# First stage of a two-layer cross-attention and mixture-of-experts kernel, rewritten without engine loops

## What is computed

```
x = x + L0_xattn(layernorm(x), ctx)          # A: cosine of every pair of tokens
    v = xn @ Wv.T + bv                       # 128 -> 64
    t = ctx @ Wt.T + bt                      # 96 -> 64, "the text side"
    out[i, j] = (v_i . t_j) / max(|v_i| |t_j|, 1e-8)
x = x + L0_ffn(layernorm(x))                 # B: routed experts
    logits = xn @ gate_w ; 8 experts in 4 groups, 2 groups, then 2 experts kept
    y = sum of the chosen experts' silu(xn @ w_gate) * (xn @ w_up) @ w_down, and a shared one
```

## Time and profile before

| what | value |
|---|---|
| median of 3 runs | 867.25 us (865.78 to 868.15) |
| profiled execution | span 862.7 us, 26300 instructions; its own time is not listed apart from the span |
| busy in the span | PE 727.4, PEld 545.5, DVE 639.6, ACT 408.4, POOL 198.2 us |
| mean granted TensorE clock | 0.931 of 2.4 GHz |
| first stage | 0 to 255.0 us of the span |

### The profile page before, as it was taken

How to read it: one execution, slowest core, us unless ns; L and a number is a source line. 1 busy time by engine, 2 the same in 40 slices (tenths; PEclk the granted TensorE clock), 3 DMA queues, 4 the chain that set the end, 5 groups by cost and what they waited for, 6 DMA issues and landing times. The chain is left out here.

```text
span 862.7 us, 26300 instructions
## 1 busy us (share of the span) xinstructions
PE 727.4 (84%) x10112; PEld 545.5 (63%) x10112; DVE 639.6 (74%) x1802; ACT 408.4 (47%) x777; POOL 198.2 (23%) x317
## 2 busy tenths in 40 slices
PE   3468898888888889889999477887759999999997
PEld 2245565555556777667787245665547888888886
DVE  7568877787868989888996577887665766666653
ACT  3123223322235656656655365665635555554553
POOL 3333222232534212330200553342011110011100
PEclk9569989998898999999999599999998999999999
DMA  4000000140034221122200000000000000000000
GB/s 103 9 22 13 23 21 21 33 88 18 24 99 100 82 78 50 53 66 79 81 15 14 4 2 5 5 4 4 5 3 2 13 13 0 12 12 12 12 13 13
DMA packets 33082, 26.43 MB, mean 31 GB/s; under 512 B 9740, under 2 KB 29912, under 8 KB 32984
## 3 DMA queue, kind: packets, MB, share of 16 engines
q1 hardware_dynamic: 29944, 24.07, 10.5%
q10 hardware_dynamic: 3040, 0.98, 0.5%
HBM read 13.51 MB, written 7.34 MB: 24 GB/s over the span
## 5 line engine op out<-in xcount | busy, mean ns | idle before, releaser
L1931 PEld LDWEIGHTS bank<-w2r,hme 128*128 128x128 f32 x1024 | 132.2, 191 | 15.6 <-ACT hme L1876 1.4
L1931 PE MATMUL bank<-w2r,hme 128*128 128x128 f32 x1024 | 135.5, 276 | 0.0
L1876 ACT ACTIVATE hme<-bank,b 128x512 f32<-128x512 f32 x128 | 86.5, 687 | 96.3 <-PE bank L97 96.3
L984 ACT ACTIVATE P<-bank 128x512 f32<-128x512 f32 x128 | 76.6, 598 | 76.2 <-PE bank L1130 75.0
L1900 DVE SCALAR_TENSOR_TENSOR Xq<-bank,wgte,Xq 128x128 f32 (+1 forms) x256 | 72.1, 344 | 51.1 <-PE bank L1931 38.3
L1056 DVE TENSOR_SCALAR bank<-bank 128x512 f32<-128x512 f32 x128 | 89.6, 700 | 15.2 <-PE bank L1121 14.4
L1064 DVE TENSOR_REDUCE mx<-bank 128x4 f32<-128x512 f32 x128 | 87.1, 681 | 1.4 <-PE bank L1104 1.3
L500 ACT ACTIVATE w2r<-bank 128x512 f32<-128x512 f32 x40 | 23.9, 597 | 114.5 <-PE bank L814 82.8
L1130 PE MATMUL bank<-mT,negsel 128*128 128x128 f16 x512 | 51.0, 223 | 13.9 <-DVE bank L1056 12.6
L95 PE MATMUL bank<-xTe,w 128*128 (+1 forms) x128 | 48.8, 381 | 5.5 <-PEq L1295 5.5
L825 PE MATMUL bank<-w_raw,hm 128*128 128x128 f32 x320 | 50.3, 308 | 2.9 <-DVE X L739 2.8
(11 more groups left out here) (382 smaller groups left out, 1785.3 us busy)
## 6 DMA issues: line engine op xcount, KB each, us to landing
cross_q<-qh SPq DMA_DIRECT2D x24, 128.0 KB
Q<-cross_q SPq DMA_DIRECT2D x8, 384.0 KB, 3.9
X<-in_x SPq DMA_DIRECT2D x8, 256.0 KB, 2.8
Xq<-X SPq DMA_DIRECT2D x32, 64.0 KB
cross_k<-kh SPq DMA_DIRECT2D x16, 128.0 KB
Yq<-Y SPq DMA_DIRECT2D x32, 64.0 KB
out_x<-Xq SPq DMA_DIRECT2D x32, 64.0 KB, 1.7
cload<-in_ctx SPq DMA_DIRECT2D x8, 192.0 KB, 2.5
```

Of the source, the lines that this page charges most:

```text
L984: act.activation(P[j][:], TB[u % 3][:], ACT.Exp, scale=SCALE).then_inc(s["p_ready"], 1)
L1876: act.activation(hm[:, p % HR], UP[p % RING][:], ACT.Gelu_apprx_tanh, bias=b1[:, p:p + 1]).then_inc(s["gelu"], 1)
L1931: last = pe.matmul(Y[f % 2][:, cols], hm[:, p % HR, cols], w2r[:, p], start=(p % 2 == 0 and i == 0), stop=(p % 2 == 1), skip_group_check=True)
```

## The change

- `sweep` and all `Fori` loops of the stage are gone. Each engine's first part (groups 0 and 1 of the cosine block, all context turns, text of groups 0 to 4, gate of group 0) is written out as a list; then `for g in range(8)` is unrolled by the program.
- The text side is separate. Raw context of all groups stays on chip (in `Xq`); its turned halves for all 8 groups and the text features of groups 0 to 4 (`EARLY = 5`) are made before the first expert product, the text of groups 5 to 7 in the loop. Text features live in the room of the second layer's K tiles. The context's sums become 32 products with a column of ones, in one place, before the first expert product.
- The text norms' diagonal is built a group ahead. The value norm is applied by ScalarE (`outer`, four scaled copies), and the clamp at 1e8 and the product with the dots become one VectorE instruction (`cosine`).
- Both normalisations go from VectorE to ScalarE as `scale * x + bias`, for which GpSimd's root computes a bias (two more small operations).
- The gate has 20 instructions instead of 23, in three parts.
- TensorE signals the gate product by itself (`g_psum`), so `silu` need not wait for the up product.
- Loads are eight pieces for x and context (1, 1, 2, 4 groups each); the second layer's weights follow at once. The weights' high half is made by VectorE. GpSimd clears the K and Q tiles and `eT`.

The core of the diff (new lines; the old ones stand in the kernel above). ScalarE:

```
+            def normalise(k, g):
+                act.wait_ge(s["rs" + k], g + 1)
...
+                for i in range(GB):
+                    b = GB * g + i
+                    last = act.activation(xn[k][:, i, :], X[:, b, :], ACT.Identity, bias=rs[k][:, 3, b:b + 1],
+                                          scale=rs[k][:, 1, b:b + 1])
+                last.then_inc(s["xn" + k], 1)
...
+            def outer(g):
...
+                    last = act.activation(wm[:, i, :], norm_bank(g)[:, col(i)], ACT.Copy, scale=rnv[:, b:b + 1])
+                last.then_inc(s["A_ready"], 1)
...
+            for g in range(G):
+                h, r, a, e = g + 2, g + 1, g + 3, g + EARLY
+                for p in range(NBLK):
+                    if p == 0:
+                        spread(g)
+                    silu(g, p)
+                    if p == 0:
+                        if g == 0:
+                            normalise("B", 1)
+                        if h < G:
+                            x_high(h)
+                        if e < G:
+                            text_out(e)
+                        if r < G:
+                            routed_high(r)
+                        if e < G:
+                            text_square(e)
+                    elif p == 1:
+                        if h < G:
+                            value_out(h)
+                        if r < G:
+                            tanh(r)
+                    elif p == 2 and a < G:
+                        normalise("A", a)
+                    elif p == 3 and h < G:
+                        outer(h)
+                    elif p == 4 and h < G:
+                        normalise("B", h)
```

VectorE, the cosine and the body of the loop over g and p:

```
+            def cosine(g):
+                dve.wait_ge(s["A_ready"], g + 1)
+                dve.wait_ge(s["dots_psum"], g + 1)
+                wf = wm[:].rearrange("p b c -> p (b c)")
+                dve.scalar_tensor_tensor(wf, wf, 1.0 / COS_EPS, turn_bank(g)[:], ALU.min, ALU.mult).then_inc(s["wm_ready"], 1)
...
+                    if p == 2:
+                        if r < G:
+                            gate(r, 0)
+                        if g > 0:
+                            add(g - 1)
+                    weigh(g, p)
+                    if p == 0:
+                        if h < G:
+                            x_low(h)
+                        if r < G:
+                            routed_low(r)
+                    elif p == 1:
+                        if a < G:
+                            stats("A", a)
+                        if e < G:
+                            text_norm(e)
+                    elif p == 2:
+                        if h < G:
+                            value_norm(h)
+                        if r < G:
+                            gate(r, 1)
+                    elif p == 3:
+                        if h < G:
+                            cosine(h)
+                        if r < G:
+                            gate(r, 2)
+                    elif p == 4 and h < G:
+                        stats("B", h)
```

GpSimd's root:

```
+            def root(k, g):
...
+                pool.tensor_scalar(rs[k][:, 0, at], mv[k][:, at, 1], 1.0, LN_EPS, ALU.mult, ALU.add)
+                pool.tensor_scalar(rs[k][:, 2, at], mv[k][:, at, 0], -1.0, None, ALU.mult).then_inc(s["eps" + k], 1)
+                pool.wait_ge(s["eps" + k], g + 1)
+                pool.tensor_tensor(rs[k][:, 1, at], rs[k][:, 0, at], half[:, 0:GB], ALU.pow).then_inc(s["pow" + k], 1)
+                pool.wait_ge(s["pow" + k], g + 1)
+                pool.tensor_tensor(rs[k][:, 3, at], rs[k][:, 2, at], rs[k][:, 1, at], ALU.mult).then_inc(s["rs" + k], 1)
```

TensorE, the end of its list and the loop:

```
+            dots(1)
+            spread_norms(1)
+            ctx_turn(4)
+            ctx_turn(5)
+            text_project(3)
+            text_squares(3)
+            text_project(4)
+            text_squares(4)
+            ctx_turn(6)
+            ctx_turn(7)
+            pe.wait_ge(s["tq_ready"], EARLY)
+            for b in range(B):
+                last = pe.matmul(G1[0:CT, b:b + 1], raw_ctx[:, b, :], ones[:, 0:1], start=True, stop=True)
+            last.then_inc(s["sum_psum"], 1)
+            for g in range(G):
+                h, r, e = g + 2, g + 1, g + EARLY
+                for p in range(NBLK):
+                    up(g, p)
+                    if p == 0:
+                        if h < G:
+                            x_turn(h)
+                        if e < G:
+                            text_project(e)
+                        down(g - 1, 3)
+                        if r < G:
+                            routed_turn(r)
+                    elif p == 1:
+                        if h < G:
+                            value_project(h)
+                        if e < G:
+                            text_squares(e)
+                        if r < G:
+                            logits(r)
+                        down(g - 1, 4)
+                    elif p == 2 and h < G:
+                        value_squares(h)
+                        dots(h)
+                    elif p == 3 and h < G:
+                        spread_norms(h)
...
+                    if p >= 2:
+                        down(g, p - 2)
```

More of the change, by code:

```diff
@@ L325, in layer0 @@
         s = room.sems(names)
         block = ctx.enter_context(nc.Block())
-        def xg(g):
-            return X[:, bass.ds(GB * g, GB), :] if not isinstance(g, int) else X[:, GB * g:GB * g + GB, :]
         P0, P1, PB, G0, G1, UP, WB, DN = bank
         GP = [G0, G1]
[L335 to L345, removed]
+        PIECES = ((0, 1), (1, 2), (2, 4), (4, 8))
@@ L395, in _ @@
[L395 to L403, removed]
+            pool.memset(half[:], -0.5)
@@ L426, in step @@
[L426 to L441, removed]
@@ new lines, in diagonal, with value_root @@
+            def diagonal(g):
+                pool.wait_ge(s["rnt_ready"], g + 1)
+                after(pool, s["rb_psum"], g)
+                for i in range(GB):
+                    last = pool.tensor_scalar(dg[:, i, :], ident[:], rnt[:, GB * g + i:GB * g + i + 1], 0.0,
+                                              ALU.mult, ALU.add)
+                last.then_inc(s["dg_ready"], 1)
+            def value_root(g):
+                pool.wait_ge(s["nv_ready"], g + 1)
+                pool.tensor_tensor(rnv[:, four(g)], n2v[:, four(g)], half[:, 0:GB], ALU.pow).then_inc(s["rn_ready"], 1)
@@ new lines, in clear @@
+            def clear(tiles):
+                for t in tiles:
+                    last = pool.memset(t.bitcast(mybir.dt.uint32), 0)
+                return last
+            pool.wait_ge(s["consts"], 3)
+            root("A", 0)
+            constants()
+            text_root(0)
+            diagonal(0)
+            value_root(0)
+            root("A", 1)
+            text_root(1)
+            residual(0)
+            clear([eT[:]]).then_inc(s["consts"], 1)
+            root("B", 0)
+            diagonal(1)
@@ new lines, in spread_norms, with routed_turn @@
+            def spread_norms(g):
+                pe.wait_ge(s["dg_ready"], g + 1)
+                pe.wait_ge(s["nv_ready"], g + 1)
+                pe.matmul(norm_bank(g)[:], ones[:], dg[:].rearrange("p b c -> p (b c)"), start=True, stop=True
+                          ).then_inc(s["rb_psum"], 1)
+            def routed_turn(g):
+                pe.wait_ge(s["xnB"], g + 1)
+                after(pe, s["eT_ready"], g)
+                if g == 0:
+                    pe.wait_ge(s["nt_ready"], FIRST)
+                for i in range(GB):
+                    last = pe.transpose(PB[:, col(i)], xn["B"][:, i, :], ident[:])
+                last.then_inc(s["xBT_psum"], 1)
@@ L2042, in build @@
         keep["expert"] = expert_tiles(room)
-        AT = [room.sb(f"AT{i}", [C, S * B], F16) for i in range(2)]
+        AT_all = room.sb("AT", [C, 2 * S * B], F16)
+        AT = [AT_all[:, S * B * i:S * B * i + S * B] for i in range(2)]
+        keep["text"] = AT_all[:].bitcast(F32)[0:DV, :]
         wp = [room.sb(f"wp{i}", [C, C], F16) for i in range(2)]
```

711 lines of the change are left out of this document (398 added, 313 removed).

## The result

The changed kernel takes 882.25 us (median of 4, 881.55 to 883.8) against 866.51 us of the kernel before in the same runs: a ratio of 1.0195, 95% interval 1.0169 to 1.022. The prediction was 878, range 860 to 893. The profiled execution has a span of 880.0 us instead of 862.7. This is the windows view after, by the same stretches as the earlier trace rows; the first instruction behind the barrier starts at 274.51, before at 254.98.

The account below looks back on a forecast made before the run. The first stage decides, its start-up and group ends paced by chains of waits: start-up 76, then 78.9, 49.2, 23.5, 22.3 and 16.0, together 265.9 against 255.0 us; span 873.6 plus 4.55 gives 878 us, range 860 to 893.

Parts of the forecast that it names:

- I take 76: Start-up: group 0's first product opens between 70 and 80 us, taken as 76, 15 more than 61.0.
- text of groups 3 and 4 (2 x 3.1): End of start-up: TensorE's two text steps, 3.1 us each, ahead of the sums and the first gate product.
- What is bought: all text up to group 4 ... out of the loop.: Return for the longer start-up: this text and all turned context leave the loop; 24.9 us a group becomes 23.3 from group 3.
- only moves work: Rival: groups 3 to 5 give back what start-up pays (+10, minus 10); kernel 867 or 868 us, chance 0.09.
- From the start of the root to the opening ... 4.4: Each group's end: GpSimd's root to the next group's first product takes 4.4 us instead of 2.6, handing back 1.8.
- I charge 1.4, 1.3, 1.3: Six groups: lower TensorE clock after idle group ends adds 1.4, 1.3, 1.3 us, giving periods 26.3, 24.6, 23.5.
- Group 5, "23.5": Group 5 in the loop: 22.2 us because it has no statistics A, 23.5 with the clock's charge.
- Groups 6 and 7, 22.3 and 16.0: End of the stage: group 6 takes 22.3 us instead of 23.5, group 7 with the barrier 16.0 instead of 16.8.
- VectorE has less slack than ScalarE ..., which speaks for the move: Six groups: VectorE busy 123.4 against ScalarE's 45.6 of 153.7 us, given as reason for moving normalisation to ScalarE.
- TensorE stays at the upper clock level: Rival, start-up and group ends: opening at 70, six groups 141.4, kernel 861 us; chance 0.21.
- ScalarE becomes the bound in order: Rival, groups: `silu` stands behind text copies, routed copy and a square; 2.5 us a group, 893 us, chance 0.13.
- 4.55: Whole kernel: the earlier median of 867.25 us stood 4.55 above the profiled span; kept in the forecast.

## Why the prediction was right, and where its sizes were off

The sign, the stretches and both causes it named were right: the start-up pays, and ScalarE's order hands back at each group's end what VectorE is relieved of. Point by point:

- **Start-up, "I take 76": 79.3.** The place of the sums, last of all, was right. Their price came out near for a reason that was not the one given: they ran at 0.50 from end to end, where the prediction's price is 14.3, and took 10.29, because a pass of these products costs 0.16 us there and not the 0.22 of the earlier trace rows; a choice between the two levels hid that. What was mis-sized is the text run ahead: "text of groups 3 and 4 (2 x 3.1)" with "a wait of about 1 for VectorE's split". The waits came to 6.3, and the sums began at 64.6 instead of 59.7 to 61.8. The sum also missed that TensorE is idle there for nearly 7 us in any case, while VectorE finishes the gate, the statistics and the splits. The sums had nothing to wait for and fit in; the texts bring waits of their own. Against the version without either, which opens at 64.42, the sums alone cost no more than VectorE's reductions (63.39), the texts alone 4.6 to 5.8 (69.02 and 70.20), both 14.9.
- **"What is bought: all text up to group 4 ... out of the loop."** In the changed kernel the last two of these texts bought 3.8 us in the six groups and cost 15.5 in the start-up. The rival "only moves work" was near in kind, but the trade was a loss, not an even one.
- **"From the start of the root to the opening ... 4.4": 4.75** (98.45 to 103.20), with ScalarE's four at 1.65 for 1.55. Right, and so is the cause, as the run with the wait alone shows.
- **The clock, "I charge 1.4, 1.3, 1.3": 2.5 a group**, by the run with the spare products. The step read one window of 3.2 us at the lower level; after the change TensorE ran some 5 to 6 us of full work at 0.50 behind an opening (131.5 to about 136; up to 109 in the group before). Group 0 was charged too, though no such wait stands ahead of it: 23.9 instead of 26.3. Groups 1 to 4 are 28.3, 27.8, 25.7 and 24.8 against 26.3, 26.3, 24.6 and 24.6. With the clock's part bought back by the spare products they are 25.2, 25.2, 23.2 and 23.2, against the 24.9, 24.9, 23.3 and 23.3 ahead of the charge: those steps were right.
- **Group 5, "23.5": 26.3.** The clock cost 2.7 there by the spare products, not the 1.3 charged. The other 1.4 is the saving "no statistics A", which did not come: with the spare products group 5 takes 23.6, no less than groups 3 and 4, because VectorE now waits 0.72 for ScalarE's `tanh` and 0.66 for the pick product instead. The mean and first statistics of the later stage (L784, L148, L152, 1.3 us in all) were left out too, but they lie mostly in the wait for the root: the group's end is 0.3 to 0.4 us longer.
- **Groups 6 and 7, 22.3 and 16.0: 21.9 and 16.5.** SP's last `q` issue (268.92 for 3.82) and VectorE's last residual add (272.64 for 0.69) end within 0.6 us of one another.
- **"VectorE has less slack than ScalarE ..., which speaks for the move"**: wrong as a reason. Giving VectorE 8 us of work back shortened the six groups by 20.9. The rule of the Trainium skill ("ScalarE: Activation LUTs", section Rules for kernel authors), to keep adds and multiplies on VectorE, agrees in sign. The price by arithmetic is small here: 1.65 us on ScalarE for the four against 1.45 on VectorE (1.12 in the kernel before). With the wait kept in ScalarE's order, the move back gained 1.6 us in the six groups and nothing in the kernel's time.
- **Rivals.** "TensorE stays at the upper clock level" did not come: 0.50 during the sums and 0.87 in the groups. In the groups it was rightly priced in kind: with the clock at 0.99 by spare products they took 144.2, where it said 141.4. "ScalarE becomes the bound in order" was wrong about the place (text copies) and near in its effect: ScalarE is 65.1 busy of 156.7, its order bound at the group's end.

The sum: start-up 3.3 over, six groups 5.1 over, groups 6 and 7 together 0.1 over, the code behind the barrier 2.2 under; and the median stands 2.25 above the span instead of 4.55. Together some 4 us. Of the six groups' 5.1, the clock is 4.3 (12.4, where 8.1 was charged). The 4.55 was no cost of its own: in every run listed with its span the time is 1.8 to 2.1 us above it, so the profiled execution of the kernel before must have been shorter than the three behind the median.

## What to carry to other kernels

Before an operation is moved to an idler engine, look at what stands behind it in that engine's order and whether it is ready earlier: a wait there is inherited by all of it, and the engine's share of busy time does not show it. If that leaves TensorE idle as long as here, 4.5 us, price the following work at the lower clock as well; here that was 2.5 us a group, more than the 1.5 by which the chain was longer. Work run ahead into a start-up is only free in a hole, and only if it waits for nobody itself: ask which engine the start-up waits for, and put independent work (here the sums) there rather than last.

## What was not expected of the hardware

- Useless products raised the speed: with 16 spare ones in each of five waits the six groups took 144.2 us instead of 156.7, at a clock of 0.99 instead of 0.87.
- The mean granted clock that a view gives for the start-up is not to be trusted in every run. With the sums on VectorE it is 0.70, with the normalisation moved as well 1.00, and yet the two start-ups are nearly equal (69.02 and 70.20). From 22 to 32 us the views give 0.51 and 1.00, while the first pass of group 1's text product takes 0.64 us in both (below, first the run with the sums alone on VectorE, then the run with both). Later, at 1.00, such a pass takes 0.38 to 0.40. The durations are the surer sign.

```profile
22.00:32.00 10.00, 7.72 (x27) 4.61 (x25) 4.22 (x14) 5.48 (x13) 4.96 (x5) 0.51 0.41 116
22.99 0.64 PE L81 MATMUL bank<-cT,wt 96*64 96x512 f16 x1
...
22.00:32.00 10.00, 7.96 (x27) 4.82 (x26) 3.22 (x12) 5.01 (x13) 4.76 (x8) 1.00 0.39 114
24.00 0.64 PE L81 MATMUL bank<-cT,wt 96*64 96x512 f16 x1
```

- Some VectorE instructions took longer where GpSimd worked at the same time: L791 took 3.39 us beside four clearings and 0.48 beside one; the four normalising instructions took 2.73 us beside clearings, 1.45 beside GpSimd's building of the diagonal, and 1.12 in the kernel before. No run here changes this alone, so the cause is not shown.
- The code behind the barrier, the same in all kernels, took 605.2 to 612.3 us in the profiled executions (before: 607.7), which blurs differences of single runs by some microseconds.
